# Scores of two attentions in a decoder layer: full-array cross scores, three-pass self-attention scores, another order of half chains

## The reference, cut to what matters

```python
x = x + attn(layernorm(x))           # causal self-attention: 16 query heads, 4 key/value heads, D = 128
x = x + xattn(layernorm(x), ctx, ctx)  # cross-attention: 32 query heads, 8 key/value heads, D = 16
x = x + ffn(layernorm(x))            # 8 experts, 2 per token, and a shared one

scores = einsum('bsgqd,btgd->bgqst', q, k) / sqrt(128)     # self-attention, causal mask, softmax
scores = einsum('bkgsd,bktd->bkgst', qh, kh) / sqrt(16)    # cross-attention, softmax
```

## Time and profile before

| | |
|---|---|
| median of 3 runs | 2172.33 us (2169.72 to 2174.08) |
| the profiled execution | 2190.71 us, of which the span is 2189.0 us |
| TensorE products busy | 2026.4 us (93%) |
| TensorE weight loads busy | 1314.4 us (60%) |
| VectorE busy | 1117.3 us (51%) |
| ScalarE busy | 901.6 us (41%) |
| GpSimd busy | 150.6 us (7%) |
| mean granted TensorE clock | 0.904 |

### The profile page before, as it was taken

How to read it: one execution, slowest core, us unless ns; L and a number is a source line. 1 busy time by engine, 2 the same in 40 slices (tenths; PEclk the granted TensorE clock), 3 DMA queues, 4 the chain that set the end, 5 groups by cost and what they waited for, 6 DMA issues and landing times.

```text
span 2189.0 us, 27241 instructions
## 1 busy us (share of the span) xinstructions
PE 2026.4 (93%) x10191; PEld 1314.4 (60%) x10191; DVE 1117.3 (51%) x2270; ACT 901.6 (41%) x1638; POOL 150.6 (7%) x233
## 2 busy tenths in 40 slices
PE   6899998999998999998999978888889699999999
PEld 4566665555554555554555432222279599999998
DVE  3445444565564566464555553434245155555564
ACT  3444432444454544544444432223322145555421
POOL 0000000000000000000000000000000511111142
PEclk9999999999999999999999875555568799999999
DMA  8333253213232132143130120000351457777643
GB/s 265 124 124 116 88 168 118 72 60 108 76 121 90 44 116 77 51 156 103 50 117 14 61 85 27 15 21 23 117 188 36 179 188 242 243 243 243 223 133 123
DMA packets 166534, 254.41 MB, mean 116 GB/s; under 512 B 8562, under 2 KB 76146, under 8 KB 166404
## 3 DMA queue, kind: packets, MB, share of 16 engines
q1 hardware_dynamic: 161284, 235.88, 31.7%
q0 software_dynamic: 5120, 16.78, 2.3%
HBM read 178.70 MB, written 73.93 MB: 115 GB/s over the span
## 4 chain that ended last, share of the span: by engine, by line
PE 80%; DVE 8%; ACT 4%; DMA 4%; issue 2%; SPq 1%; POOL 0%; DVEq 0%
PE ps L57 41%; PE ps L993 8%; PE ps L64 7%; PE ps L1006 7%; PE ps L944 7%; PE ps L918 5%; PE ps L978 4%; DVE xmax L1460 3%; ACT xp L1248 2%; DMA rows_x<-w_raw 2%; DMA q<-q_parts 1%; PE ps L917 1%; ACT probs L1183 1%; DVE nmax L1371 1%; DMA q_parts<-both 1%
## 5 line engine op out<-in xcount | busy, mean ns | idle before, releaser
L1460 DVE TENSOR_REDUCE xmax<-ps 128x1 f32<-128x512 f32 x512 | 352.3, 688 | 354.6 <-PE ps L978 351.2
L1248 ACT ACTIVATE xp<-ps 128x1024 f32<-128x1024 f32 x256 | 262.2, 1024 | 298.8 <-PE ps L993 298.5
L978 PE MATMUL ps<-k,q 48*128 48x512 f32 x512 | 297.5, 581 | 63.8 <-DVE xmax L1460 37.0
L993 PE MATMUL ps<-q,k 50*128 50x512 f32 x512 | 272.4, 569 | 19.1 <-ACT xp L1248 18.2
L1183 ACT ACTIVATE probs<-ps,nmax 128x128 f32<-128x128 f32 (+3 forms) x256 | 135.0, 527 | 373.9 <-DVE nmax L1371 373.1
L993 PEld LDWEIGHTS ps<-q,k 50*128 50x128 f32 x512 | 105.2, 223 | 232.0 <-issue 181.1
L918 PE MATMUL ps<-k_t,q_t 128*128 128x128 f32 (+3 forms) x512 | 195.9, 465 | 0.0
L978 PEld LDWEIGHTS ps<-k,q 48*128 48x128 f32 x512 | 108.5, 212 | 140.5 <-DVE xmax L1460 107.3
L1006 PE MATMUL ps<-xp,vx 128*32 128x512 f32 x1024 | 175.4, 765 | 1.1 <-ACT xp L1248 1.1
L1371 DVE TENSOR_REDUCE nmax<-ps 128x1 f32<-128x128 f32 (+3 forms) x256 | 124.7, 487 | 91.6 <-PE ps L918 91.1
L944 PE MATMUL ps<-pt,v_s 128*128 128x128 f32 (+3 forms) x512 | 154.7, 446 | 0.0
(11 more groups left out here) (182 smaller groups left out, 3261.1 us busy)
## 6 DMA issues: line engine op xcount, KB each, us to landing
w_raw<-in_w_t SPq DMA_DIRECT2D x54, 704.0 KB
w_raw<-in_w_t SPq DMA_DIRECT2D x27, 768.0 KB
wh<-w_parts SPq DMA_DIRECT2D x12, 1536.0 KB, 6.5
wl<-w_parts SPq DMA_DIRECT2D x12, 1536.0 KB, 10.2
woh<-w_parts SPq DMA_DIRECT2D x12, 1024.0 KB, 5.4
wol<-w_parts SPq DMA_DIRECT2D x12, 1024.0 KB, 7.9
q_parts<-both SPq DMA_DIRECT2D x48, 256.0 KB, 2.9
q<-q_parts SPq DMA_DIRECT2D x128, 96.0 KB
```

The source lines that it names most:

```text
L978: pe.matmul(ps[:, XS, :], q3[head_rows(h), m % KEPT, h // 2, i * P:(i + 1) * P], k3[head_rows(h), m % KEPT, :], start=True, stop=True).the ...
L993: ins = pe.matmul(ps[:, XST + hf, :], k3[head_rows_max(h), m % KEPT, j * P:(j + 1) * P], q3[head_rows_max(h), m % KEPT, h // 2, :], start= ...
L1248: act.activation(xp[:, n % KEPT_XP], ps[:, XST:XST + 2, :], ACT.Exp, scale=X_SCALE).then_inc(s_xe, 1)
L1460: dve.tensor_reduce(xmax[:, m % 2, h, i:i + 1], ps[:, XS, :], AX_X, ALU.max, negate=True).then_inc(s_xmax, 1)
```

## The change

Cross scores: the odd head's 48 rows move to partitions 48 to 95, and the maxima's rows of both heads to 96 to 99. `k3` gets a copy for each of the two heads with zeros in the other head's rows, so one product takes 96 (`most`) or 100 (`alike`) rows, of which only one head's count. `q3` and `k3` keep three items instead of four, `both` one buffer instead of two. Within a step the two `alike` stand together behind the turns, one `most` stays early and the other follows the first half chain; `xpv` comes for two j at a time, behind `pv`.

Self-attention scores: ScalarE writes only the high parts `qh`, `kh`; VectorE adds the low parts `ql`, `kl` (`take_low`); `score` makes three fp32r passes, and the mask product is fp32r too. Half chains, turned rows and reloads get other steps; `give` goes head by head, so that its first half needs two heads only. `ah` and `al` keep four heads instead of five.

```diff
-KEPT, KEPT_XP = 4, 4
+KEPT, KEPT_XP, KEPT_VX = 3, 4, 4
...
+PART_STEPS = [0, 1, 2, 2, 3, 3, 4, 4] + [5 + n * 11 // 12 for n in range(12)]
...
-            step = UNITS * g + 2 + p * UNITS // len(parts)
-            at(step, "part", "part", *part)
+            step = UNITS * g + PART_STEPS[p]
+            at(step, "late" if p == 1 else "part", "part", *part)
...
-            at(UNITS * g + UNITS - 1, "end", "values", g + 1)
+            at(UNITS * g + 12, "end", "values", g + 1)
...
-                at(UNITS * g + 2, "first", "reload", "in", g + 1)
+                at(UNITS * g, "first", "reload", "in", g + 1)
...
-            at(UNITS * g + 9, "first", "reload", "out", g)
+            at(UNITS * g + 5, "first", "reload", "out", g)
...
-                at(g + UNITS + 2 + t, "first", "row", 1, b + 1, t)
-                at(g + UNITS + 2 + t, "end", "turn_row", 1, b + 1, t)
+                at(g + UNITS + (0, 2, 3, 4)[t], "first", "row", 1, b + 1, t)
+                at(g + UNITS + (0, 2, 3, 4)[t], "end", "turn_row", 1, b + 1, t)
...
-        at(g + 8, "end", "turn_ctx", b)
-        at(g + 8, "first", "spread", b)
-        at(g + 9, "end", "root", b)
+        at(g + 5, "end", "turn_ctx", b)
+        at(g + 5, "first", "spread", b)
+        at(g + 6, "end", "root", b)
-            at(g + 10 + t, "first", "row", 2, b, t)
-            at(g + 10 + t, "end", "turn_row", 2, b, t)
+            at(g + (7, 8, 10, 11)[t], "first", "row", 2, b, t)
+            at(g + (7, 8, 10, 11)[t], "end", "turn_row", 2, b, t)
...
-            at(s + r, "a", "most", m, r, 0)
-            at(s + r, "b", "most", m, r, 1)
-            at(e + r, "a", "alike", m, r, 1)
-            at(e + r, "b", "alike", m, r, 0)
+            at(s + r, "cross", "most", m, r, 0)
+            at(s + r, "cross", "most", m, r, 1)
+            at(e + r, "cross", "alike", m, r, 0)
+            at(e + r, "cross", "alike", m, r, 1)
         for j in range(TOK_TILES):
-            at(e + 2 * j + 2, "xpv", "xpv", m, j)
+            at(e + 4 * (j // 2) + 4, "xpv", "xpv", m, j)
...
         head, tail = step["part"][:1], step["part"][1:]
-
-        low = sorted(step["b"], key=lambda op: op[0] == "most")
-        ops += (step["first"] + step["a"] + step["pv"] + step["turn"] + head + low + step["xpv"] + step["end"] + tail)
+        most, alike = ([op for op in step["cross"] if op[0] == kind] for kind in ("most", "alike"))
+        ops += (step["first"] + most[:1] + step["pv"] + step["xpv"] + step["turn"] + alike + head + most[1:] + step["end"]
+                + step["late"] + tail)
...
 def head_rows(h):
-    return slice(h % 2 * HALF, h % 2 * HALF + X_ROWS)
...
+    return slice(h % 2 * X_ROWS, h % 2 * X_ROWS + X_ROWS)
+def max_rows(h):
+    return slice(2 * X_ROWS + h % 2 * X_MAX, 2 * X_ROWS + h % 2 * X_MAX + X_MAX)
...
     def chain_free(c):
                 before = CHAINS[c - 1]
-                if before[0] == "in":
+                if before in SPLIT_QK:
+                    pe.wait_ge(s_ql, SPLIT_QK.index(before) + 1)
+                elif before[0] == "in":
...
     def give(dst, g, t, half):
-                if half == 0 and t == 0:
-                    pe.wait_ge(s_al, QPG * g + QPG)
+                if t == 0:
+                    pe.wait_ge(s_al, QPG * g + QPG // HALVES * (half + 1))
...
     def score(u):
-                pe.matmul(ps[:, S_BANK, i * P:w], ident_b[:, :], mask[:, :], start=True, stop=True)
-                pe.matmul(ps[:, S_BANK, 0:w], q_t[:, h, i * P:w], k_t[:, g % 2, 0:w],
-                          start=False, stop=True, skip_group_check=True).then_inc(s_s, 1)
+                pe.matmul(ps[:, S_BANK, i * P:w], ident_r[:, :], mask[:, :], start=True, stop=True)
+                for q, k in ((qh, kh), (qh, kl), (ql, kh)):
+                    ins = pe.matmul(ps[:, S_BANK, 0:w], q[:, h, i * P:w], k[:, g % 2, 0:w],
+                                    start=False, stop=True, skip_group_check=True)
+                ins.then_inc(s_s, 1)
...
     "most":
-                    pe.matmul(ps[:, XS, :], q3[head_rows(h), m % KEPT, h // 2, i * P:(i + 1) * P],
-                              k3[head_rows(h), m % KEPT, :], start=True, stop=True).then_inc(s_xs, 1)
+                    rows = slice(0, 2 * X_ROWS)
+                    pe.matmul(ps[:, XS, :], q3[rows, m % KEPT, h // 2, i * P:(i + 1) * P],
+                              k3[rows, m % KEPT, hf, :], start=True, stop=True).then_inc(s_xs, 1)
...
+            def take_low(g, n, src):
+                name = PIECES[n]
+                if name == "v":
+                    return
+                dve.wait_ge(s_q, TAKEN.index(("in", g, n)) + 1)
+                if name == "k":
+                    low(kl[:, g % 2, :], kh[:, g % 2, :], src).then_inc(s_ql, 1)
+                else:
+                    h = int(name[1])
+                    dve.scalar_tensor_tensor(ql[:, h, :], src, ATT_SCALE, qh[:, h, :].bitcast(F32), ALU.mult,
+                                             ALU.subtract).then_inc(s_ql, 1)
...
     "part", on VectorE:
+                    elif op[1] == "in" and op[4] == HALVES - 1:
+                        take_low(op[2], op[3], ps[:, G_BANK, :])
```

More of the change, by code:

```diff
@@ L89 @@
 N_STEP = exp_step(ITEMS - 1) + 10
+PART_STEPS = [0, 1, 2, 2, 3, 3, 4, 4] + [5 + n * 11 // 12 for n in range(12)]
 def step_plan():
-    steps = [{"first": [], "a": [], "pv": [], "part": [], "b": [], "xpv": [], "turn": [], "end": []}
+    steps = [{"first": [], "pv": [], "part": [], "late": [], "cross": [], "xpv": [], "turn": [], "end": []}
              for _ in range(N_STEP)]
@@ L385, in build @@
         s_low = sem("s_low")
-        s_so = [sem(f"s_so{n}") for n in range(2)]
+        s_so = sem("s_so")
         s_kq = [sem(f"s_kq{n}") for n in range(2)]
@@ L593, in _ @@
                 sp.dma_start(res[:, b * TOK_TILES:(b + 1) * TOK_TILES, :], x_v[b]).then_inc(s_x[b], 16)
-            sp.wait_ge(s_one, 1)
-            sp.dma_start(ones_rows, o_t[0:X_MAX, :]).then_inc(s_rows1, 16)
-            sp.wait_ge(s_rows1, 16)
+            sp.wait_ge(s_one, 2)
+            for n in range(2):
+                sp.dma_start(k_rest[n:n + 1, :], o_t[32 * n:32 * n + 1, :]).then_inc(s_rows1, 16)
+            sp.wait_ge(s_rows1, 32)
             for hf in range(2):
-                for slot in range(KEPT):
-                    sp.dma_start(k3[hf * HALF + X_ROWS:hf * HALF + X_ROWS + X_MAX, slot, :].bitcast(F32), ones_rows)\
+                for n, at in enumerate((max_rows(hf), max_rows(1 - hf), head_rows(1 - hf))):
+                    rows = at.stop - at.start
+                    sp.dma_start(k3[at, :, hf, :].bitcast(F32),
+                                 k_rest[min(n, 1):min(n, 1) + 1, :].unsqueeze(1).to_broadcast([rows, KEPT, SEQ]))\
                         .then_inc(s_rows1, 16)
@@ L648, in _ @@
                         stored = len([x for x in STAGED if x[1 if x[0] == "turn_ctx" else 2] <= b])
-                        for par in range(2):
-                            sp.wait_ge(s_so[par], 48 * ((stored + 1 - par) // 2))
+                        sp.wait_ge(s_so, 48 * stored)
                     if m >= KEPT:
@@ L904, in give @@
                 toks = slice(t * P, (t + 1) * P)
-                pairs = [(a[:, (QPG * g + h) % (QPG + 1), toks], w[:, h, :])
-                         for a, w in ((ah, woh), (ah, wol), (al, woh)) for h in range(QPG)]
+                pairs = [(a[:, h, toks], w[:, h, :])
+                         for h in range(QPG) for a, w in ((ah, woh), (ah, wol), (al, woh))]
                 return products(pe, dst, pairs[half * N_PART:(half + 1) * N_PART], half == 0, half == HALVES - 1)
@@ L1217, in _ @@
                     act.wait_ge(s_t, TURNS.index(op) + 1)
[L1218 to L1220 removed]
+                    if n:
+                        act.wait_ge(s_so, 48 * n)
+                    act.copy(both[:, 0, :], ps[:, T_BANK, :]).then_inc(s_high, 1)
                 elif op in TURNS:
@@ L1400, in _ @@
                 low(xl[at], xh[at], ps[:, FIRST_BANKS[t], :].rearrange("p (c n) -> p c n", c=KC)).then_inc(s_xl, 1)
-            for n in range(2, len(PIECES)):
+            for n in range(2, 4):
                 split("in", 0, n)
+            take_low(0, 0, ps[:, G_BANK, :])
+            for n in range(4, len(PIECES)):
+                split("in", 0, n)
+            take_low(0, 1, ps[:, O_BANK, :])
             maxima(0)
@@ L1447, in _ @@
                     dve.wait_ge(s_high, n + 1)
-                    low(both[:, n % 2, 1, :], both[:, n % 2, 0, :], ps[:, T_BANK, :]).then_inc(s_low, 1)
+                    low(both[:, 1, :], both[:, 0, :], ps[:, T_BANK, :]).then_inc(s_low, 1)
                 elif op[0] == "turn_row":
```

106 lines of the change are left out of this document (53 added, 53 removed).

## The result

The changed kernel takes 2219.1 us (median of 4 runs, 2214.7 to 2221.7) against 2173.2 us for the kernel before (median of 4): ratio 1.021, 95% interval 1.019 to 1.024. It is slower by 46 us.

A forecast was written before the change was run, and what follows sets the result against it. TensorE was taken as the bound, its time being what it issues plus new holes. Terms -20 + 4 + 66 + 16 - 32 + 11 - 10 - 6 = +29 us; 2172.3 + 28 = 2200 us, range 2135 to 2245.

The forecast's parts named there:

- other holes: Cross-attention steps with no half chain between score and next score: TensorE waits for the maximum, 1.6 us a group, +17 us.
- exp waits: Stage with both attentions: the wait for the exponential of the score pair goes, 11.9 us in all.
- groups 0 to 4: Groups without cross scores: chains wait longer for ScalarE and VectorE, 3.3 us a group, +16 us (0 to +26).
- Part 1: Cross scores beside self-attention: full-array pairs cost 0.46 us against 0.52, 326 pairs, -20 us.
- Part 2: Self-attention scores in three passes: 2.7 us a head against 2.61, +6 us (-13 to +31), entered as +4.
- Part 3: VectorE's low parts delay maxima in groups 5 to 14, +61; with other holes and exp waits +66 us.
- Part 4: Batch starts: earlier rows end the wait for loads of q, -32 us; one buffer for `both` costs +11.
- Part 5: Cross-attention alone: items of 30 us against 30.3, high clock a third of the time, -10 us; group 15 and after, -6.
- the flicker: Cross-attention alone: clock changes around the items, put at some 10 us within the -10 us term.
- Rival (a): Cross-attention alone runs at 2.4 GHz, items of 24 us, -54 instead of -10: 2156 us; chance 0.25.
- Rival (b): Low parts hide: the holes in groups 5 to 14 are filled, +61 becomes about 0: 2139 us; chance 0.12.
- Rival (c): Narrow self-attention passes are dear and the clock stays down, +25 and +20 more: 2245 us; chance 0.15.

The follow-up runs named there:

- e3: Kernel before with only the cross scores changed to the full array, three buffers for k and q: 2143.2 us (0.9863).
- e6: e3 plus the change's moved half chains, reloads and value transposes, rows staged still earlier, and one staging buffer: 2162.0 us (0.9951).
- e2: The changed kernel with self-attention scores as one fp32 product instead of three passes, no low parts: 2172.4 us (1.0004).
- the first experiment: The changed kernel with VectorE making a low part behind the step's second maximum wherever that follows at once: 2181.7 us (1.0055).

## Why the forecast was right, and where it was wrong

Slower by 28 us was forecast (the terms add up to 29), slower by 46 was measured, within the range, but not for all the reasons given. The terms beside what the experiments measured, by the medians and by the ledger's attention stages alone (all but the last column), in us:

```
term of the forecast                                  forecast  medians  attention stages  from
full array and cross-attention alone (parts 1, 5)       -36      -29        -31          e3 - before
earlier rows, one staging buffer (part 4)               -21      +19        +10          e6 - e3
order inside a step (other holes +17, exp waits -12)     +5      +10        +25          e2 - e6
three passes, low parts, groups 0 to 4 (+4, +61, +16)   +81      +47        +49          after - e2
sum                                                     +29      +47        +54
```

(The experiments add up in one order, from 2172.4 us; the two middle rows depend on it. The attention stages start from the second profile of before; the last stage takes 8 us back.)

The forecast's sign is right because its largest term is right in kind, but its closeness is partly luck: the low parts were priced too high, and the moved half chains and the new order too low. One group shows it. From 81.0 us the forecast comes to 86.0 (-1.9 for the pairs, +0.4 for the passes, +6.1 and +1.6 for the holes, -1.2 for the exponentials), and 85.6 was measured; but the steps on the way are 79.0 (`e3`, full array), 80.9 (`e6`, half chains moved), 81.8 (`e2`, order inside a step) and 85.6 (after, split scores): -2.0, +1.9, +0.9 and +3.8.

- **Part 1 right.** 0.52 against 0.46 us a pair: a group lost 2.0 us, as 32 x 0.06 has it. The drain of the Trainium skill (TensorEngine Tiling (Array Packing), Key Properties) agrees in sign: the full-array pair costs exactly its two streams of 0.23. That the 0.09 in front of the old pair is this drain and nothing else, no run separates.
- **Part 2 mis-sized.** Forecast 2.7 us a head, not below 2.4. Measured: 0.39 + 0.47 + 0.63 + 0.80 = 2.29, from mask products of 0.06 and passes of 0.11, 0.12, 0.17 and 0.23 (the first pass of each unit 0.05 longer beyond 128 columns). With the 0.14 of the mask product behind transposes it is 2.37, still below the 2.61 that the forecast reckoned for the old scores. That is -15 to -20 instead of +6. The low end of 2.4 was no bound, because it gave the mask product the 0.11 of the 8-column products.
- **Part 3, the mechanism right, the size not.** The place, the order and the time (H + 2.26 against H + 2.34) are as forecast. Measured waits in a group: 1.40, 1.39, 1.30, 0.95 in the four steps and 0.39 in one other, 5.4 us, against 6.1 + 1.6. The step that failed is the comparison: the whole hole was charged to the low part, though a hole of 0.4 stands there without it (the 0.41 above; in `e2`, without low parts, four waits of 1.3 us in all). Moving the low part gives 4.0 us a group back, not 6.1.
- **Groups 0 to 4 right in sum**: +18.4 against +16. The waits for `ql` are there (8.8 us, 19 times, 0.7 at most), but 7.7 of the 18.4 us stay when the low parts go (`e2`), all that the forecast gave to the moved half chains there (5 x 1.5 us) before it took off what falls into idle time.
- **Part 4 wrong in sign.** It counted what the earlier rows take away, and at nothing what the moved half chains and reloads do: 44 us, a part of it through a longer wait for the same loads. It looked at the earlier reload only for its own use, not for the loads of q that it now follows. In after that wait is 16.8 us, 5.8 at most, where the forecast had none above 1 us. The +11 for the single buffer was +1.3: ScalarE's wait is real, but TensorE had work meanwhile.
- **Part 5**: items of some 30.5 us and a clock that changes within each, as forecast; its mean of 0.67 over the stage (1281 to 1643 us) means the high level for a third of the time, as assumed. Four windows of 4 us, one after the other, in the trace of after:

```profile
1427.00:1431.00 4.00, 4.00 (x17) 0.74 (x17) 1.09 (x2) 0.00 (x0) 0.00 (x0) 0.50 0.02 4
1431.00:1435.00 4.00, 3.00 (x12) 1.63 (x8) 1.98 (x3) 1.78 (x3) 0.00 (x0) 0.85 0.02 4
1435.00:1439.00 4.00, 2.54 (x5) 1.12 (x4) 2.62 (x5) 1.43 (x2) 0.00 (x0) 0.58 0.02 4
1439.00:1443.00 4.00, 3.11 (x7) 1.43 (x7) 1.91 (x9) 1.02 (x1) 1.01 (x1) 0.50 0.04 4
```

The weighing runs at the low level, the high one follows it, and the loop of scores behind it does not hold it. The gain of 10 us did not come. The forecast's own figures give 8.5 x 0.3 = 2.6 us; the rest, "the flicker", stood on no row. Full array alone gains 6 us in this stage, with the change's order on top of it the stage is 14 longer, and in after one batch's wait of 5.8 us stays in it. Rival (a) had the price right and the condition wrong: the clock does not stay high by the full rows, but where two more products a score keep it there, an item takes 25.0 us, close to its 24.
- **Rival (b)** fails by the fixed order, as argued; the first experiment shows that another order makes most of it true. **Rival (c)** fails in both parts: a pass of 128 columns takes 0.11, not 0.21, and the items take 30.5 us, not the 32.7 of a clock that stays down.
- **The profiled execution**: 14 of its 18 us above the median lay in the last stage, whose code the change does not touch; carrying the sum over as a difference was the right thing to do.

## What to carry to other kernels

When an engine gets a new instruction, look at what stands behind it in its queue: here the same instruction cost 37 us ahead of a maximum and little behind it, with VectorE idle over 40% of a group (49.0 busy of 85.6 us). Charge a new wait only with what exceeds the wait that stood there before. When work is moved, price the steps it leaves as well as those it goes to: the distance between two other events, here the stores of a batch and its first use, is measured in those steps. And compare stages before totals: a stage with unchanged code moved by up to 15 us here with what came before it.

## What the hardware showed that was not expected

- Split products of 128 columns on 128 rows cost 0.11 us from start to start, the mask product ahead of them 0.06 (0.14 behind transposes), with each weight load (0.19) beside the product before it.
- Work that nobody needs shortened the kernel by 39 us: with two more products a score the granted clock stayed at 1.00 where it was 0.60, an item took 25.0 us instead of 30.2 to 31.2, and nothing waited for the added products.
- The same kernel takes 2172.4 to 2172.8 us on three chips and 2188.1 on a fourth. The one trace from there, of another kernel, has 18.7 us of idling put down to issue; the traces known to be from the other three have no such row.
